# The output projection of a two-layer attention kernel in matmuls of 256 instead of 512 columns

## What is computed

```
for layer in (L0, L1):
    xn  = layernorm(x) * g_in
    q   = xn @ Wq            # 512 -> 16 heads x 64 = 1024 columns
    k,v = xn @ Wkv           # one head of 64 for all; a null key and value are put in front
    sim = q k^T + bias       # causal, with a padding mask; L1 normalises q and k
    out = softmax(sim) v     # 128 rows x 1024
    x   = x + layernorm(out @ Wo) * g_out      # Wo: 1024 x 512
```

## Time and profile before

| | |
|---|---|
| median of 3 runs | 2467.25 us (2465.68 to 2468.71) |
| the profiled execution | 2467.19 us |
| its span, first to last instruction | 2465.4 us |
| busy: PE, PEld | 2383.4 us (97%), 2087.3 us (85%) |
| busy: DVE, ACT, POOL | 1642.0 (67%), 1631.4 (66%), 902.9 us (37%) |
| mean granted clock of TensorE | 0.987 of 2.4 GHz |

### The profile page before, as it was taken

How to read it: one execution, slowest core, us unless ns; L and a number is a source line. 1 busy time by engine, 2 the same in 40 slices (tenths; PEclk the granted TensorE clock), 3 DMA queues, 4 the chain that set the end, 5 groups by cost and what they waited for, 6 DMA issues and landing times.

```text
span 2465.4 us, 53983 instructions
## 1 busy us (share of the span) xinstructions
PE 2383.4 (97%) x16801; PEld 2087.3 (85%) x16801; DVE 1642.0 (67%) x4685; ACT 1631.4 (66%) x6621; POOL 902.9 (37%) x1691
## 2 busy tenths in 40 slices
PE   1699999999999999999999999999999999999998
PEld 0588888888888888888888888888888888888887
DVE  5566766766766766766766766766766766766766
ACT  2466666666666666666666666666666666666665
POOL 0333433433433433433433433433433433433432
PEclk7799999999999999999999999999999999999999
DMA  6101101101101101101101101101101101101101
GB/s 200 40 29 46 41 28 45 41 28 45 41 28 45 41 28 45 41 28 45 41 28 45 41 28 45 41 28 45 41 28 45 41 28 45 41 28 45 41 24 36
DMA packets 94907, 102.24 MB, mean 41 GB/s; under 512 B 47616, under 2 KB 49696, under 8 KB 94880
## 3 DMA queue, kind: packets, MB, share of 16 engines
q1 hardware_dynamic: 90192, 99.90, 13.1%
q10 hardware_dynamic: 4688, 2.01, 0.4%
HBM read 48.89 MB, written 16.79 MB: 27 GB/s over the span
## 4 chain that ended last, share of the span: by engine, by line
PE 96%; DVE 0%; ACT 0%; issue 0%; POOL 0%; POOLq 0%; DVEq 0%
PE psum L351 33%; PE psum L431 29%; PE psum L417 10%; PE psum L385 10%; PE psum L397 6%; PE psum L368 5%; PE psum L338 3%; PE psum L359 1%; ACT probs L514 0%; DVE probs L631 0%; DVE neg_max L638 0%; DVE x_lo L582 0%; POOL weights L738 0%; ACT x_hi L473 0%; DVE x_out L666 0%
## 5 line engine op out<-in xcount | busy, mean ns | idle before, releaser
L738 POOL TENSOR_TENSOR weights<-probs,den_inv 128x256 f32<-128x256 f32 (+3 forms) x1024 | 466.3, 484 | 1468.7 <-DVE den_inv L644 1460.8
L514 ACT ACTIVATE probs<-probs,neg_max 128x129 f32<-128x129 f32 (+3 forms) x2048 | 717.2, 353 | 373.4 <-DVE neg_max L638 373.4
L725 POOL TENSOR_TENSOR masked_bias<-bias,pad_neg 128x516 f32<-128x516 f32 (+3 forms) x512 | 392.9, 800 | 15.3 <-POOL pad_neg L721 9.0
L631 DVE TENSOR_TENSOR probs<-psum,masked_bias 128x324 f32<-128x324 f32 x512 | 225.4, 482 | 257.8 <-PE psum L385 257.8
L514 ACT ACTIVATION_READ_ACCUMULATOR probs<-probs,neg_max 128x1 f32 x2048 | 387.0, 189 | 0.0
L351 PE MATMUL psum<-w_hi,x_hi 128*128 128x384 f32 x1536 | 337.9, 342 | 4.4 <-DVE x_lo L582 4.4
L351 PE MATMUL psum<-w_hi,x_lo 128*128 128x384 f32 x1536 | 330.3, 337 | 0.0
L351 PE MATMUL psum<-w_lo,x_hi 128*128 128x384 f32 x1536 | 329.9, 337 | 0.0
L351 PEld LDWEIGHTS psum<-w_hi,x_hi 128*128 128x128 f32 x1536 | 273.0, 190 | 16.7 <-DVE x_lo L582 5.3
L385 PEld LDWEIGHTS psum<-keys,q_t 64*128 64x128 f32 x4096 | 238.6, 188 | 49.4 <-issue 49.4
L351 PEld LDWEIGHTS psum<-w_lo,x_hi 128*128 128x128 f32 x1536 | 273.2, 189 | 0.0
(11 more groups left out here) (111 smaller groups left out, 3219.0 us busy)
## 6 DMA issues: line engine op xcount, KB each, us to landing
xa<-in_x_dram SPq DMA_DIRECT2D x64, 256.0 KB, 2.6
x_res<-in_x_dram SPq DMA_DIRECT2D x64, 256.0 KB, 2.6
out_dram<-x_out SPq DMA_DIRECT2D x64, 256.0 KB, 2.1
x_in<-x SPq DMA_DIRECT2D x62, 256.0 KB, 2.3
x_res<-x_in SPq DMA_DIRECT2D x62, 256.0 KB, 2.3
raw<-in_L_cond_Wq_dram SPq DMA_DIRECT2D x8, 512.0 KB, 7.5
raw<-in_L_cond_Wo_dram SPq DMA_DIRECT2D x8, 256.0 KB, 5.1
raw<-in_L_cond_Wout_dram SPq DMA_DIRECT2D x8, 256.0 KB, 7.2
```

Source lines behind the costliest of these rows:

```text
L514: x_ = nc.scalar.activation(s, s, ACT.Exp, bias=neg_max[:, g, k, e:e + 1], accum_out=den[:, g, k, e:e + 1])
L631: a = nc.vector.tensor_tensor(probs[:, 2 * c + e, :], SB[c][e][:, 0:ROW], masked_bias[u.layer][:, 2 * c + e, :], ALU.add)
L725: m = nc.gpsimd.tensor_tensor(block(masked_bias[u.layer], b), block(bias[u.layer], b), pad_neg[u.layer][:, 0:WIDTH[b]].unsqueeze(1).to_bro ...
L738: m = nc.gpsimd.tensor_tensor(places[b], block(pairs(probs, g // 2), b)[:, :, 1:1 + n], den_inv[:, g, k, :].unsqueeze(2).to_broadcast([P, ...
```

## The change

Each of the 24 matmuls of a unit's output projection, 128 x 512 columns, becomes two of 256 columns, one into the left and one into the right half of the bank, in turns, both with the same stationary piece. The order of the pieces and passes is kept. [...] `skip_group_check` silences a check of the language and makes no instruction.

```
--- before.py
+++ after.py
@@ -428,8 +428,12 @@
                         wait(pe, o_lo_done[b], u.done)
                 os, ws = ((o_hi, wo_hi), (o_hi, wo_lo), (o_lo, wo_hi))[p]
                 for j in range(PAIRS):
-                    m = nc.tensor.matmul(Y[:, 0:D], os[:, j * P:(j + 1) * P], ws[u.layer][:, j, :],
-                                         start=(p == 0 and j == 0), stop=(p == 2 and j == PAIRS - 1))
+
+                    for half in range(2):
+                        cols = slice(half * D // 2, (half + 1) * D // 2)
+                        m = nc.tensor.matmul(Y[:, cols], os[:, j * P:(j + 1) * P], ws[u.layer][:, j, cols],
+                                             start=(p == 0 and j == 0 and half == 0),
+                                             stop=(p == 2 and j == PAIRS - 1 and half == 1), skip_group_check=True)
                 if p == 2:
                     m.then_inc(y_done, 1)
```

## The result

The changed kernel takes 2477.46 us (median of 5 runs, 2476.1 to 2478.62), the one before 2466.26 us beside it (5 runs). The ratio is 1.0042, with a 95% interval of 1.0029 to 1.0055, so the kernel is slower by 11 us; a gain was forecast. The range of 2428 to 2497 us held the time. The span of the profiled execution went from 2465.4 to 2475.4 us.

A forecast was written before the change was run, and what follows sets the result against it. The prediction took PE as the bound, with the output projection 29% of the waits chain. Spacing of 114.5 ns gave -0.130 us a unit, -16.6 us over 128 units: 2467.2 to 2451 us, range 2428 to 2497 us.

The forecast's parts named there:

- the surcharge at 256 columns: Output projection: time above the bare 106.7 ns of a half matmul, whose spacing was taken as 114.5 ns.
- the first two: Estimates of the 256-column spacing: a straight line through both known widths, 112.0 ns, or surcharge per column, 115.5 to 117.2 ns.
- The line through two widths: Straight line through the spacings at 512 and 384 columns, 61 ns per 128 columns, giving 112.0 ns at 256.
- the sum: Output projection per unit: 48 x 114.5 = 5.496 us against 5.626, -0.130 us, x 128 = -16.6 us.
- the stall with each matmul: Rival: handover between consecutive output matmuls costs 13.2 ns each or more; spacing 119.9 ns, 2484 us; chance 0.20.
- The small fixed cost: Rival: each output matmul has a few ns of its own, the rest per column; 118.7 ns, 2476 us; chance 0.10.
- the hindrance between the two reads: Sign for an output spacing above 117 ns: the two operand reads hinder each other when both are continuous.
- a cost with each matmul: Other sign for an output spacing above 117 ns: a fixed cost sits at each handover between matmuls.
- Every half has its own load: Each half matmul of the output projection was counted with a weight load: 24 more loads per unit.
- The load hides: Output projection: a load of about 107 ns just fits beside the 106.7 ns that 256 columns take.
- The forecast's 107 ns from the scores: Time of one load, from the scores' 26 loads at 53.6 ns each, 107 per row half.
- L351 stays at 173 ns a matmul: Claim that the untouched 384-column matmuls of L351 keep their spacing of 173 ns.

The follow-up runs named there:

- e2_m96: The changed kernel with stationary pieces of 96 columns in place of 128, except a unit's first; 2468.5 us.
- e9_m_256: The changed kernel with stationary pieces of 64, 32 and 128 columns in passes 0, 1 and 2 (first piece 128); 2470.5 us.
- e3_widths: The kernel before with output matmuls of 128, 192 and 448 columns in passes 0, 1 and 2 (first 512), other columns left out; 2316.4 us.
- e1_blocks: The changed kernel with each pass doing all left halves of the bank, then all right halves; 2476.14 us, ratio 1.0035 to the kernel before.
- e6_noacc: The kernel before with passes 0 and 2 overwriting in place of adding, and pass 2 split into 2 x 256 columns; 2470.08 us.
- e7_bf16: The kernel before with passes 0 and 2 reading both operands' upper two bytes as bfloat16, and pass 2 split into 2 x 256; 2457.86 us.

## Why the prediction was wrong

**The failed step** is the size of the surcharge at 256 columns: "From 512 to 384 the surcharge fell faster than the columns, which speaks for the first two", and so 114.5 ns. The line through two widths was read as a slope that goes on downwards, to 8 ns at 256. The table shows nearly none there: 384, 320 and 256 columns pay 13, 13 and 12 ns per matmul, and the 512 belongs to the widest ones, which pay 17 to 21. Twice 12 is 24, more than 21. In the terms of the sum, 48 x 118.8 = 5.70 us against 5.626 is +0.076 us a unit, +10 us in all, where -16.6 us was forecast. That it gives the measured difference to the microsecond is in part luck: the matmuls at 117.3 ns make the output projection itself cost 7.8 us, and 2.0 us come from L351, which the sum put at nothing.

**Of the rivals** the stall with each matmul had the mechanism: one surcharge per matmul, paid twice, at L351's size. It asked for 119.9 ns and 2484 us; the surcharge is a little under L351's, 12 ns. It got a chance of 0.20. The small fixed cost, at 0.10, had the number (118.7 ns, 2476 us) with another story: the rest of the surcharge by columns. By that story 384 columns would have 16.5 ns on top, and they have 13; 448 would have 19, and have 14 in early slots, though 18 in late ones. No run shows its fixed 3 ns per matmul: the runs show 12 to 14 ns at 256 to 448 columns in early slots. Of the two reasons that the prediction gave in advance for a spacing above 117, the hindrance between the two reads is small at most (e2_m96, e9_m_256), and a cost with each matmul is what the widths show.

**What held.** The chain, not the busy time, gave the cost before (234 ns) and after. Every half has its own load. The load hides: its own rate is 111 ns (e3_widths), below 118.8, and shortening it by a quarter gives back less than 1 ns a matmul (e2_m96). The forecast's 107 ns from the scores, where two row halves load in turns, was some 4 ns low for full rows. No wait came in. That L351 stays at 173 ns a matmul held in 37 of the 60 late slots; in the others its 36 matmuls take 6.36 us, 177 ns each.

**What stays open** is what the 12 to 14 ns are, why 480 columns and more pay up to 21, and why an untouched L351 has slots that are 0.11 us longer. It is not the turns (e1_blocks, still 117.3 and 118.8 ns), not adding in PSUM (e6_noacc, 118.8 ns), and to the greater part not the load (e9_m_256, 114 to 117.5 ns with a quarter of it). L351 took 320 ns at a granted clock of 0.50 and takes 173.2 ns at 1.00, 13.2 more than half of that. With two-byte operands the surcharge was smaller, 13 ns at 512 columns and 8 at 256 (e7_bf16), where the shorter loads (97 ns against 188) may be the reason; no run shows their part by itself.

## What to carry to other kernels

Here PE was the bound, and splitting its matmul paid a surcharge per matmul once more. Where that may be so, compare the surcharge of the whole with twice that of the half, and measure the half: two widths don't make a slope. A matmul whose columns take less than the load (here 192 columns in a four-byte type, 80 ns against 111) is paid at the load's price, and both uneven splits tried here were worse than the even one. The spacing comes from groups in order of time, where a nanosecond counts: here one ns per matmul is 6 us. Look at more than one pass of a loop, and at the neighbours of what was changed: the passes of the changed kernel differ, and a fifth of its loss stands on a line that the change did not touch.

## What was not expected of the hardware

- The surcharge over one column per cycle at full clock is 12 to 14 ns for 256 to 448 columns (18 at 448 in late slots), and 17 to 21 ns for 480 to 512.
- The same kernel has matmul groups at 117.3 and at 118.8 ns. In nearly every pass of e1_blocks the early slot is the faster one (5.63 us for 48) and the late one the slower (3.80 for 32, with L351 at 6.36). The changed kernel has passes like that and passes the other way round (5.70 for 48, 3.76 for 32, L351 at 6.24), by turns for most of the run. What picks the level isn't known.
- A load of 128 columns on 128 rows in this type can follow another after 111 ns (e3_widths), and one of a quarter of its columns shortens a 256-column spacing by 1 to 5 ns only (e9_m_256).
